# A Mamba scan on one Trainium2 core: decays double-buffered in SBUF, the product with B single-buffered in PSUM

## The chip, the cores and the metric

The kernel runs on 1 core of one Trainium2 chip. The metric is the device time of one execution in microseconds (us). Durations in the text come from one profiled execution; the time is given as the median of three runs.

## The reference, cut to what matters

The network has four parts. The change lies in the third, a selective scan over 4 batches of length 1024 with 512 channels (4 blocks of 128) and 16 states:

```python
dt = softplus(dbl[..., :16] @ W_dt.T + b_dt)
A = -exp(A_log)
def step(h, inp):                       # one position
    dA = exp(dt_t[:, :, None] * A)      # the decay
    h = h * dA + (dt_t * u_t)[:, :, None] * B_t[:, None, :]
    y = einsum('bcs,bs->bc', h, C_t)
ys = scan(step, h0, ...)
y = (ys + u * D_skip) * silu(z)
out = y @ W_out.T
```

`x` here has batch 4, 1024 positions and 256 features. Before the scan come a Fourier-kernel attention block with a gated mix, after it a mixture of 8 experts with layer norm; the change touches neither.

## The kernel before, in words

Two phases follow each other in one program: `phase_a` (attention and mix) and `phase_me` (scan, then experts). In `phase_me` channels lie on the 128 partitions and the 1024 positions along the free axis. One **step** is one state of one block of 128 channels of one batch, so there are 4 batches x 4 blocks x 16 states = 256 steps, numbered n. All engines run their own queues in order and meet at semaphores. A step is:

- **ScalarE, `decay` (L1318 to L1324)**: dA = exp(dt x A) for the 128x1024 tile, into one PSUM buffer `dA`. It waits for `h_ok >= n`, that is, for the scan of step n-1, because that scan reads the one buffer.
- **VectorE, `times_b` (L1610 to L1616)**: dB = du x (row of B, broadcast over the partitions), du read from PSUM, dB written to one of two buffers in SBUF (`late`). It waits for the B row's load, for `du_ok`, and for `h_ok >= n-1`, the scan two steps back.
- **VectorE, `scan` (L1618 to L1623)**: h = scan(dA, dB), into one of three buffers in SBUF. It waits for dA, dB and (from the fourth step) for the product that last read its output buffer.
- **GpSimd, `times_c` (L1144 to L1150)**: pr = h x (row of C).
- **TensorE, `add_state` (L1755 to L1762)**: adds pr onto Y in PSUM by an identity matmul; between these it does `half_job`s, the projections of the same and the next batch (table `FILL`).
- **SyncE, `rows_in` (L1059 to L1067)**: two DMAs a step that broadcast a row of B and a row of C over the partitions; the B row's buffer is freed by `dB_ok`.

The order on VectorE is written out: scan(n), times_b(n+1), scan(n+1), with one `gate` (L1625 to L1630, Y x silu(z)) per block of channels after times_b of the block's third step.

Once per block of 16 steps (t counts the 16 blocks; m is the block within a batch, s the step within the block):

- **GpSimd, `drive` (L1136 to L1142)** makes dt x u for the next block in SBUF (`dus`), at s = 10, 13, 13 and 14 for m = 0 to 3 (table `DRIVE`), behind `times_c` and the work in `besides` (`rate` L1134, `silu` L1130 and, in batches 1 and 2, an indirect DMA at every odd step, L1197).
- **ScalarE, `drive_out` (L1326 to L1330)** copies it to PSUM as `du`, where `times_b` reads it. It waits for `dus_ok`, and for `dB_ok >= 16 t`, the last `times_b` of the block before. It stands at s = 15, after that step's decay and before that step's other jobs.
- **ScalarE, `skip_term` (L1332 to L1338)** writes D x u into Y, at s = `SKIP` = 2, after the decay and after the gate of the block before.
- `block0` to `block3` (L1340 to L1452) are ScalarE's other jobs by step: evacuations of TensorE's half jobs (L1266 to L1292) and the parts of silu and softplus (L1302 to L1316). They stand behind that step's decay.

PSUM holds four tensors of 128x1024 float32: Q0 (dA), Q1 (du), Q2 (the half jobs' two halves), Q3 (Y).

Of the kernel before, what the change touches and what calls it, by code (L numbers as in the profile page):

```python
# [9 lines left out]
ALU = mybir.AluOpType  # L10
ACT = mybir.ActivationFunctionType
AX = mybir.AxisListType

B, L, D = 4, 1024, 256
# [810 lines left out]
DI, NS, DC, DR = 512, 16, 4, 16  # L825
KI = DI // P
STEPS = KI * NS
NBB, NCB, NH, NU = 3, 4, 3, KI + 1
# [65 lines left out]


DRIVE = (10, 13, 13, 14)
SKIP = 2

NTILE = 39
GROUP = 3  # L900
# [4 lines left out]
def phase_me(nc, g):  # L905

    AT = half_jobs()
    with ExitStack() as ctx:
        def sb(name, shape, dt=F32):
            return ctx.enter_context(nc.sbuf_tensor(name, shape, dt))  # L910

        def sem(name):
            return ctx.enter_context(nc.semaphore(name))
# [3 lines left out]
        late = sb("late", [P, 10 * L])  # L917

        def part(of, at, shape, dt=F32):

            n = int(np.prod(shape))
            v = of[:, at:at + n]
            v = v if dt is F32 else v.bitcast(dt)
            if len(shape) == 2:
                return v.rearrange("p (a b) -> p a b", b=shape[1])
            if len(shape) == 3:
                return v.rearrange("p (a b c) -> p a b c", b=shape[1], c=shape[2])
            return v
# [6 lines left out]
        bb = part(rows, NCB * L, [NBB, L])  # L935
        soft = part(rows, 7 * L, [L])
        h = part(late, 0, [NH, L])
        pr = part(late, 3 * L, [NH, L])
        dB = part(late, 6 * L, [2, L])
        dt = part(late, 8 * L, [2, L])  # L940

        w_bc, w_dt, acol, taps, vecs, one, ident = (g[n] for n in ("w_bc", "w_dt", "acol", "taps", "vecs", "one", "ident_m"))
# [54 lines left out]

        Q = [ctx.enter_context(nc.psum_tensor(f"m_Q{i}", [P, 2, CH], F32)) for i in range(4)]
        pT1, pM1, pM2, pT2 = Q
        dA, du, _, Y = (q[:, :, :].rearrange("p a b -> p (a b)") for q in Q)  # L1000
        X = [Q[2][:, i, :] for i in range(2)]
        R0, R1 = Q[3][:, 0, :], Q[3][:, 1, :]

# [7 lines left out]
        dA_ok = sem("m_dA_ok"); dB_ok = sem("m_dB_ok")  # L1011
        h_ok = sem("m_h_ok"); pr_ok = sem("m_pr_ok"); y_full = sem("m_y_full"); yg_ok = sem("m_yg_ok")
# [16 lines left out]
        with nc.Block() as block:  # L1029
# [220 lines left out]
            def _(ac):  # L1250
                A = nc.scalar.activation
# [66 lines left out]
                def decay(b, i):  # L1318
                    n = b * STEPS + i
                    m = i // NS  # L1320
                    ac.wait_ge(dt_ok, b * KI + m + 1)
                    if n:
                        ac.wait_ge(h_ok, n)
                    A(dA[:, :], dt[:, (b * KI + m) % 2, :], ACT.Exp, scale=acol[:, m, i % NS:i % NS + 1]).then_inc(dA_ok, 1)  # L1324

                def drive_out(t):  # L1326
                    ac.wait_ge(dus_ok, t + 1)
                    if t:
                        ac.wait_ge(dB_ok, t * NS)
                    A(du[:, :], dus[:, :], ACT.Identity).then_inc(du_ok, 1)  # L1330

                def skip_term(t):  # L1332

                    if t:
                        ac.wait_ge(yg_ok, t)
                    else:
                        ac.wait_ge(rt_ok, 1)
                    A(Y[:, :], u[:, t % NU, :], ACT.Identity, scale=vecs[:, 1, t % KI:t % KI + 1]).then_inc(skip_ok, 1)  # L1338

                def block0(b, s):  # L1340
                    t = b * KI
                    if b == 0:
                        if s in (1, 2):
                            evacuate(0, "z", 0, s - 1)
                        elif s in (6, 7, 8, 9, 10, 11):
                            evacuate(0, "z", (s - 4) // 2, s % 2)
                        for first, z in ((2, 0), (8, 1), (11, 2), (14, 3)):
                            if 0 <= s - first < 3:
                                sigmoid(0, "z", z, s - first)
                    if s == 0 and b:  # L1350
                        sigmoid(b, "z", 3, 2)
                    elif s in (4, 5):
                        evacuate(b, "dt", 1, s - 4)
                    elif s == 6:
                        softplus(t + 1, 0)
                    if s in (7, 9, 11, 13) and b:
                        evacuate(b - 1, "out", 0, (s - 7) // 2)
                    if s == 7:
                        softplus(t + 1, 1)
                    if s in (14, 15) and b + 1 < B:  # L1360
                        evacuate(b + 1, "x", 0, s - 14)

                def block1(b, s):
                    t = b * KI + 1
                    more = b + 1 < B
                    if s == 0 and b == 0:
                        sigmoid(0, "z", 3, 2)
                    if s in (5, 6):
                        evacuate(b, "dt", 2, s - 5)
                    if more:  # L1370
                        if s == 1:
                            evacuate(b + 1, "conv", 0, 0)
                        elif s == 4:
                            evacuate(b + 1, "conv", 0, 1)
                            sigmoid(b + 1, "conv", 0, 0)
                        elif s in (7, 8):
                            evacuate(b + 1, "z", 0, s - 7)
                        elif s == 9:
                            evacuate(b + 1, "x", 1, 0)
                            sigmoid(b + 1, "conv", 0, 1)  # L1380
                        elif s == 10:
                            evacuate(b + 1, "x", 1, 1)
                            sigmoid(b + 1, "conv", 0, 2)
                        elif s == 11:
                            sigmoid(b + 1, "z", 0, 0)
                        elif s == 12:
                            evacuate(b + 1, "conv", 1, 0)
                            sigmoid(b + 1, "z", 0, 1)
                        elif s == 13:
                            sigmoid(b + 1, "z", 0, 2)  # L1390
                        elif s == 14:
                            evacuate(b + 1, "conv", 1, 1)
                            sigmoid(b + 1, "conv", 1, 0)
                        elif s == 15:
                            evacuate(b + 1, "z", 1, 0)
                            sigmoid(b + 1, "conv", 1, 1)
                    if s == 7:
                        softplus(t + 1, 0)
                    elif s == 8:
                        softplus(t + 1, 1)  # L1400
# [63 lines left out]
                for b in range(B):  # L1464
                    for i in range(STEPS):
                        decay(b, i)
                        m, s = divmod(i, NS)
                        if s == NS - 1 and b * KI + m + 1 < B * KI:
                            drive_out(b * KI + m + 1)
                        if s == SKIP:  # L1470
                            skip_term(b * KI + m)
                        if m == 0:
                            block0(b, s)
                        elif m == 1:
                            block1(b, s)
                        elif m == 2:
                            block2(b, s)
                        elif b + 1 < B:
                            block3(b, s)
# [51 lines left out]
            def _(dv):  # L1531
                v_ = nc.vector
# [77 lines left out]
                def times_b(n):  # L1610
                    t = n // NS
                    dv.wait_ge(b_in[n % NBB], 16 * (n // NBB) + 16)
                    dv.wait_ge(du_ok, t + 1)
                    if n >= 2:
                        dv.wait_ge(h_ok, n - 1)
                    v_.tensor_tensor(dB[:, n % 2, :], du[:, :], bb[:, n % NBB, :], ALU.mult).then_inc(dB_ok, 1)  # L1616

                def scan(n):  # L1618
                    dv.wait_ge(dA_ok, n + 1)
                    dv.wait_ge(dB_ok, n + 1)  # L1620
                    if n >= NH:
                        dv.wait_ge(pr_ok, n - NH + 1)
                    v_.tensor_tensor_scan(h[:, n % NH, :], dA[:, :], dB[:, n % 2, :], 0.0, ALU.mult, ALU.add).then_inc(h_ok, 1)  # L1623

                def gate(t):  # L1625
                    dv.wait_ge(y_full, (t + 1) * NS)
# [4 lines left out]

                route()
                times_b(0)
                for n in range(B * STEPS):
                    scan(n)
# [284 lines left out]
```

## Time and profile before

| | |
|---|---|
| median of 3 runs | 2482.49 us (2481.26 to 2482.85) |
| the profiled execution's own time | 2483.26 us |
| its span, first to last instruction | 2481.1 us |
| scan stage, first to last scan's start | 1063.8 to 2020.4 us |
| busy in the span | PE 1995.6, DVE 1646.6, ACT 1264.7, POOL 1082.0 us |

DVE is VectorE, ACT ScalarE, POOL GpSimd, PE TensorE, SP SyncE; L1623 is line 1623 of the kernel. A row of the timeline gives start, duration, engine, line, operation and tiles (`out<-in`); brackets give the idle time before it and who ended it. A wait is put down to the one that came last, and only idle time over a small threshold is named. Tiles are named by their memory: `late` and `rows` are SBUF tensors that are shared by many buffers, `m_Q` is any of the four PSUM tensors.

### The profile page before, as it was taken

The page shows a single profiled execution, that of the slowest core. Times are in us where ns is not written, and L with a number is a line of the kernel's source. Part 1 is how long each engine was busy: PE and PEld are TensorE (multiplying, and loading weights), DVE is VectorE, ACT ScalarE, POOL GpSimd, SP SyncE. Part 2 cuts the span into 40 slices and gives each one's busy share as a digit, 9 for nine tenths or more (in the row PEclk, how much of TensorE's full clock was granted, in tenths as well). Part 3 has the DMA queues.
Part 4 walks back from the last instruction along what each step waited for, and adds up shares of the span by engine and source line. Part 5 has one row for each costly group of instructions (what it writes and reads, how often), then busy time and mean ns, then how long its engine had stood idle before and what let it go on. Part 6 is the DMA issues. An engine that isn't in the chain of part 4 may idle for free. (4 is left out here: it accounts for less than half of the span.)

```text
span 2481.1 us, 24432 instructions
## 1 busy us (share of the span) xinstructions
PE 1995.6 (80%) x7355; PEld 1006.8 (41%) x7371; DVE 1646.6 (66%) x2303; ACT 1264.7 (51%) x1703; POOL 1082.0 (44%) x605
## 2 busy tenths in 40 slices
PE   4789778967886796879978988998776669989883
PEld 3326433633463253323324332433232236655552
DVE  4754576366726533379989998999899962225663
ACT  3962586268527731466654665466544424434441
POOL 3001201020111010178888898989877751213553
PEclk9899899989999998989998998999999999999996
DMA  7410730073016202488888888988889972223444
GB/s 173 108 34 0 184 72 18 13 189 70 0 38 164 53 34 62 7 286 287 291 288 284 300 275 279 298 289 276 273 274 345 328 255 79 90 89 90 122 122 131
DMA packets 183457, 407.69 MB, mean 164 GB/s; under 512 B 49937, under 2 KB 78865, under 8 KB 182114
## 3 DMA queue, kind: packets, MB, share of 16 engines
q1 hardware_dynamic: 171298, 375.31, 50.3%
q0 software_dynamic: 12032, 30.82, 4.3%
q8 instruction: 63, 1.03, 0.2%
q14 instruction: 64, 0.52, 0.1%
HBM read 360.50 MB, written 49.70 MB: 165 GB/s over the span
## 5 line engine op out<-in xcount | busy, mean ns | idle before, releaser
L1150 POOL TENSOR_TENSOR late<-late,rows 128x1024 f32<-128x1024 f32 x256 | 603.2, 2361 | 153.6 <-DVE late L1623 148.4
L1760 PE MATMUL m_Q<-late,ident_m 128*128 128x512 f32 x1024 | 527.7, 646 | 170.7 <-POOL late L1150 118.2
L1623 DVE TENSOR_TENSOR_SCAN late<-m_Q,late 128x1024 f32<-128x1024 f32 x256 | 586.3, 2290 | 47.5 <-ACT m_Q L1324 19.5
L1324 ACT ACTIVATE m_Q<-late,acol 128x1024 f32<-128x1024 f32 x256 | 286.0, 1117 | 373.9 <-DVE late L1623 373.7
L1760 PEld LDWEIGHTS m_Q<-late,ident_m 128*128 128x128 f32 x1024 | 193.1, 201 | 478.2 <-POOL late L1150 281.7
L1616 DVE TENSOR_TENSOR late<-m_Q,rows 128x1024 f32<-128x1024 f32 x256 | 307.3, 1200 | 40.5 <-ACT m_Q L1330 34.5
L424 DVE SCALAR_TENSOR_TENSOR early<-early,work 128x1024 f32<-128x1024 f32 x128 | 156.0, 1219 | 123.1 <-ACT early L570 122.3
L1507 ACT ACTIVATE late<-m_Q,e_b1c 128x128 f32<-128x128 f32 x312 | 89.2, 369 | 202.4 <-PE m_Q L1825 173.2
L302 POOL TENSOR_TENSOR xk<-kr 128x1024 f32<-128x1024 f32 x8 | 15.0, 1894 | 397.3 <-DVE kr L438 397.3
L570 ACT ACTIVATE early<-work,rnd 128x1024 f32<-128x1024 f32 x128 | 141.7, 1110 | 63.2 <-PE work L722 60.0
L1837 PE MATMUL m_Q<-rows,late 128*128 x624 | 155.8, 393 | 21.3 <-ACT late L1507 12.5
L277 POOL TENSOR_TENSOR qkh<-early,qkh 128x1024 bf16<-128x1024 f32 x16 | 33.9, 2129 | 284.4 <-ACT qkh L533 284.4
L1816 PE MATMUL m_Q<-early,late 128*128 x312 | 151.8, 610 | 2.6 <-ACT late L1491 2.0
L578 ACT ACTIVATE early<-early,halfpi 128x1024 f32<-128x1024 f32 x128 | 146.0, 1141 | 0.0
L577 ACT ACTIVATE early<-early 128x1024 f32<-128x1024 f32 x128 | 134.8, 1053 | 21.1 <-DVE early L427 21.0
L1837 PEld LDWEIGHTS m_Q<-rows,late 128*128 128x128 f32 x624 | 112.7, 190 | 52.2 <-issue 39.9
L1728 PE MATMUL m_Q<-early 128*128 128x512 f32 x256 | 122.5, 605 | 4.8 <-ACT m_xi L1266 4.0
L465 DVE TENSOR_TENSOR s<-work,s 128x1024 f32<-128x1024 f32 x8 | 9.8, 1225 | 172.9 <-PE work L646 172.9
L646 PE MATMUL work<-w,qkh 128*128 128x256 f32 x512 | 112.6, 381 | 10.9 <-ACT qkh L594 10.9
L1733 PE MATMUL m_Q<-m_xi,early 128*128 128x512 f32 x256 | 119.7, 601 | 0.0
L1651 DVE TENSOR_TENSOR late<-m_Q,m_u 128x256 f32<-128x256 f32 x39 | 16.6, 425 | 144.4 <-PE m_Q L1837 105.2
L808 PE MATMUL work<-x2T,w 128*128 128x512 f32 x256 | 111.6, 594 | 1.0 <-ACT x2T L510 1.0
(226 smaller groups left out, 3086.5 us busy)
## 6 DMA issues: line engine op xcount, KB each, us to landing
rows<-bc_s SPq DMA_DIRECT2D x512, 512.0 KB, 5.5
stack<-st_s SPq DMA_DIRECT2D x64, 384.0 KB, 5.8
st_s<-qkh SPq DMA_DIRECT2D x128, 96.0 KB, 2.4
r_s<-late SPq DMA_DIRECT2D x39, 256.0 KB
stack<-st_s SPq DMA_DIRECT2D x32, 256.0 KB, 6.7
xin<-in_x SPq DMA_DIRECT2D x4, 1024.0 KB, 9.9
xres<-in_x SPq DMA_DIRECT2D x4, 1024.0 KB, 7.5
mx_s<-s SPq DMA_DIRECT2D x4, 1024.0 KB, 4.5
```

The costliest lines, as they stand in the source:

```text
L424: v_.scalar_tensor_tensor(fs[:, s % 3, :], fs[:, s % 3, :], ROUND, slot(b, *job)[:, :], ALU.subtract, ALU.subtract).then_inc(rr_ok, 1)
L570: A(fs[:, s % 3, :], slot(b, *job)[:, :], ACT.Identity, bias=rnd[:, :]).then_inc(turns_ok, 1)
L577: A(fs[:, s % 3, :], fs[:, s % 3, :], ACT.Sin, scale=-TURN).then_inc(feat_ok, 1)
L578: A(fc[:, s % 3, :], fc[:, s % 3, :], ACT.Sin, scale=-TURN, bias=halfpi[:, :]).then_inc(feat_ok, 1)
L1150: nc.gpsimd.tensor_tensor(pr[:, n % NH, :], h[:, n % NH, :], cb[:, n % NCB, :], ALU.mult).then_inc(pr_ok, 1)
L1324: A(dA[:, :], dt[:, (b * KI + m) % 2, :], ACT.Exp, scale=acol[:, m, i % NS:i % NS + 1]).then_inc(dA_ok, 1)
L1616: v_.tensor_tensor(dB[:, n % 2, :], du[:, :], bb[:, n % NBB, :], ALU.mult).then_inc(dB_ok, 1)
L1623: v_.tensor_tensor_scan(h[:, n % NH, :], dA[:, :], dB[:, n % 2, :], 0.0, ALU.mult, ALU.add).then_inc(h_ok, 1)
L1728: ins = mm(dst[:, :], w_in[:, k, (m + KI * (kind == "z")) * P:(m + KI * (kind == "z") + 1) * P], half(xT[:, k, :], c), start=(k == 0), sto ...
L1760: ins = mm(half(Y, c), ident[:, :], half(pr[:, n % NH, :], c), start=False, stop=(n % NS == NS - 1), skip_group_check=True)
L1816: ins = mm(pM1[:, q % 2, :], xsT[:, q % 2, k * P:(k + 1) * P], e_w1[:, k, bass.ds(e * HE, HE)], start=(k == 0), stop=(k == KD - 1))
L1837: ins = mm(pM2[:, q % 2, 0:D], hT[:, q % 2, k * P:(k + 1) * P], e_w2[:, k, bass.ds(e * D, D)], start=(k == 0), stop=(k == HE // P - 1 and ...
```

## The change

The decays get two buffers in SBUF, the place where dB had its two; dB gets the one PSUM buffer where the decays were. The waits follow the buffers. `skip_term` moves from s = 2 to s = 3, and `drive_out` from s = 15 (after the block's last decay) to s = 0 of the next block (after that block's first decay).

```diff
-SKIP = 2
+SKIP = 3
...
-        dB = part(late, 6 * L, [2, L])
+        dA = part(late, 6 * L, [2, L])
...
-        dA, du, _, Y = (q[:, :, :].rearrange("p a b -> p (a b)") for q in Q)
+        dB, du, _, Y = (q[:, :, :].rearrange("p a b -> p (a b)") for q in Q)
...
                     ac.wait_ge(dt_ok, b * KI + m + 1)
-                    if n:
-                        ac.wait_ge(h_ok, n)
-                    A(dA[:, :], dt[:, (b * KI + m) % 2, :], ACT.Exp, scale=acol[:, m, i % NS:i % NS + 1]).then_inc(dA_ok, 1)
+                    if n >= 2:
+                        ac.wait_ge(h_ok, n - 1)
+                    A(dA[:, n % 2, :], dt[:, (b * KI + m) % 2, :], ACT.Exp, scale=acol[:, m, i % NS:i % NS + 1]).then_inc(dA_ok, 1)
...
                         m, s = divmod(i, NS)
-                        if s == NS - 1 and b * KI + m + 1 < B * KI:
-                            drive_out(b * KI + m + 1)
+                        if s == 0 and b * KI + m:
+                            drive_out(b * KI + m)
                         if s == SKIP:
                             skip_term(b * KI + m)
...
                     dv.wait_ge(du_ok, t + 1)
-                    if n >= 2:
-                        dv.wait_ge(h_ok, n - 1)
-                    v_.tensor_tensor(dB[:, n % 2, :], du[:, :], bb[:, n % NBB, :], ALU.mult).then_inc(dB_ok, 1)
+                    if n:
+                        dv.wait_ge(h_ok, n)
+                    v_.tensor_tensor(dB[:, :], du[:, :], bb[:, n % NBB, :], ALU.mult).then_inc(dB_ok, 1)
...
-                    v_.tensor_tensor_scan(h[:, n % NH, :], dA[:, :], dB[:, n % 2, :], 0.0, ALU.mult, ALU.add).then_inc(h_ok, 1)
+                    v_.tensor_tensor_scan(h[:, n % NH, :], dA[:, n % 2, :], dB[:, :], 0.0, ALU.mult, ALU.add).then_inc(h_ok, 1)
```

## Rows read from the trace of the kernel before

**Rows 1.** Groups by line, whole span: count, busy us, mean ns, idle before, releaser
```profile
L1623 DVE TENSOR_TENSOR_SCAN late<-m_Q,late 128x1024 f32<-128x1024 f32 x256 | 586.3, 2290 | 47.5 <-ACT m_Q L1324 19.5
L1616 DVE TENSOR_TENSOR late<-m_Q,rows 128x1024 f32<-128x1024 f32 x256 | 307.3, 1200 | 40.5 <-ACT m_Q L1330 34.5 <-DMA rows<-bc_s 6.0
L1324 ACT ACTIVATE m_Q<-late,acol 128x1024 f32<-128x1024 f32 x256 | 286.0, 1117 | 373.9 <-DVE late L1623 373.7
```

**Rows 2.** The line of the scan: shortest, median, longest; first and last start
```profile
L1623 DVE TENSOR_TENSOR_SCAN late<-m_Q,late x256: 2283/2291/2293, 1063.8 to 2020.4; 128x1024 f32<-128x1024 f32 x128
```

**Rows 3.** Timeline of an ordinary step: start us, duration us
```profile
1408.52 1.20 DVE L1616 TENSOR_TENSOR late<-m_Q,rows 128x1024 f32<-128x1024 f32 x1
1408.70 1.12 ACT L1324 ACTIVATE m_Q<-late,acol 128x1024 f32<-128x1024 f32 x1 [0.77 <-DVE late L1623]
1409.85 2.29 DVE L1623 TENSOR_TENSOR_SCAN late<-m_Q,late 128x1024 f32<-128x1024 f32 x1
1412.06 1.20 DVE L1616 TENSOR_TENSOR late<-m_Q,rows 128x1024 f32<-128x1024 f32 x1
1413.39 2.29 DVE L1623 TENSOR_TENSOR_SCAN late<-m_Q,late 128x1024 f32<-128x1024 f32 x1
```

**Rows 4.** Timeline of a step whose B row came late
```profile
1105.21 1.12 ACT L1324 ACTIVATE m_Q<-late,acol 128x1024 f32<-128x1024 f32 x1 [0.96 <-DVE late L1623]
1107.81 1.23 DVE L1616 TENSOR_TENSOR late<-m_Q,rows 128x1024 f32<-128x1024 f32 x1 [2.70 <-DMA rows<-bc_s]
1109.13 2.29 DVE L1623 TENSOR_TENSOR_SCAN late<-m_Q,late 128x1024 f32<-128x1024 f32 x1
```

**Rows 5.** Timeline in the first phase: the second waits for the first
```profile
300.71 1.22 DVE L424 SCALAR_TENSOR_TENSOR early<-early,work 128x1024 f32<-128x1024 f32 x1 [1.30 <-ACT early L570]
301.96 0.69 DVE L427 TENSOR_SCALAR early<-early 128x1024 int32<-128x1024 int32 x1
```

**Rows 6.** Groups by line and form, ScalarE and VectorE
```profile
L1330 ACT ACTIVATE m_Q<-dus 128x1024 f32<-128x1024 f32 x16 | 16.4, 1028 | 33.9 <-POOL dus L1142 33.6
L1308 ACT ACTIVATE early<-early 128x1024 f32<-128x1024 f32 x32 | 33.5, 1046 | 0.1
L396 DVE SCALAR_TENSOR_TENSOR early<-work,cols,qkh 128x1024 f32<-128x1024 f32 x16 | 20.5, 1283 | 54.0 <-ACT qkh L529 36.2 <-issue 17.8
```

**Rows 7.** Timeline before block 7 (steps 107 to 112), GpSimd, ScalarE, VectorE
```profile
1466.66 2.39 POOL L1150 TENSOR_TENSOR late<-late,rows 128x1024 f32<-128x1024 f32 x1 [1.14 <-DVE late L1623]
...
1478.40 2.37 POOL L1142 TENSOR_TENSOR dus<-late,m_u 128x1024 f32<-128x1024 f32 x1
1480.80 1.03 ACT L1330 ACTIVATE m_Q<-dus 128x1024 f32<-128x1024 f32 x1 [2.49 <-POOL dus L1142]
1481.91 1.23 DVE L1616 TENSOR_TENSOR late<-m_Q,rows 128x1024 f32<-128x1024 f32 x1 [1.28 <-ACT m_Q L1330]
1484.56 2.29 DVE L1623 TENSOR_TENSOR_SCAN late<-m_Q,late 128x1024 f32<-128x1024 f32 x1 [1.42 <-ACT m_Q L1324]
```

**Rows 8.** Timeline before block 8 (steps 125 to 128)
```profile
1534.32 2.36 POOL L1150 TENSOR_TENSOR late<-late,rows 128x1024 f32<-128x1024 f32 x1 [1.15 <-DVE late L1623]
...
1542.46 2.34 POOL L1142 TENSOR_TENSOR dus<-late,m_u 128x1024 f32<-128x1024 f32 x1
1545.95 1.23 DVE L1616 TENSOR_TENSOR late<-m_Q,rows 128x1024 f32<-128x1024 f32 x1 [4.73 <-ACT m_Q L1330]
1547.97 2.29 DVE L1623 TENSOR_TENSOR_SCAN late<-m_Q,late 128x1024 f32<-128x1024 f32 x1 [0.79 <-ACT m_Q L1324]
```

**Rows 9.** Timeline before block 6 (steps 94 to 96)
```profile
1415.30 0.69 ACT L1271 ACTIVATE m_u<-m_Q,vecs 128x512 f32<-128x512 f32 x1 [1.95 <-PE m_Q L1733]
1424.09 2.29 DVE L1623 TENSOR_TENSOR_SCAN late<-m_Q,late 128x1024 f32<-128x1024 f32 x1 [1.28 <-ACT m_Q L1324]
```

**Rows 10.** Timeline, steps 79 and 80: the half job that a copy at s = 15 waits for
```profile
1357.44 1.88 PE L1728 MATMUL m_Q<-early 128*128 128x512 f32 x4
```

**Rows 11.** Waits of VectorE from 1060 to 2030 us: total, times, longest
```profile
DVE late L1623 <- ACT m_Q L1324: 19.5, 25, 2.4
```

## The prediction

> **What bounds the kernel now.** I read three views: the groups by line, the timeline of VectorE beside its suppliers, and the waits. The groups first [rows 1]: the 256 scans of 2290 ns and the 256 `times_b` of 1200 ns are 893.6 us of VectorE work, in a stage of 2020.4 - 1063.8 = 956.6 us from the first to the last scan's start [rows 2]. VectorE is the engine of this stage. The difference is what a change of waits can touch: 16 gates of about 0.92 us each in the chain, and small gaps and stalls.
>
> The timeline of an ordinary step shows more than the groups' idle column [rows 3]. A scan starts at 1409.85 and lasts 2.29 us, but the next `times_b` starts 2.21 us after it: it waits for nothing that is recent, and starts 0.08 us before the scan's end. The next scan starts 1.33 us after the `times_b` start, though that lasted 1.20. So a step takes 3.54 us (3.535 over several), and 211 of the 255 intervals between scans show this to 0.02 us. Two waits end nearly together ahead of the scan: the decay's end (1408.70 + 1.12 = 1409.82, and the scan starts 0.03 later), and `times_b`'s own completion. ScalarE cannot start the decay before the last scan ended, which is why it waits 373.7 us [rows 1].
>
> Which of the two holds the scan is told by the one step whose B row was late [rows 4]. There the decay had ended at 1106.33, far ahead, and the scan still started 1109.13 - 1107.81 = 1.32 us after `times_b`, that is 0.09 us after the end of that 1.23 us instruction. VectorE waiting for its own last result costs 0.09 us here. With the decay out of the way the leg from `times_b` to scan therefore stays at 1.32 us. It gives back 0.01 us a step, not 0.13.
>
> **The change part by part.**
>
> *Decays in two buffers.* The decay of step n may now start after scan n-2. ScalarE comes off the ordinary step; it gives 0.01 us there, by the paragraph above. Its own length is hidden either way (writing SBUF instead of PSUM costs it about 0.02: 1046 ns SBUF to SBUF against 1028 ns into PSUM [rows 6]). Where a decay was late because of ScalarE's other jobs, the lead of a whole step covers it. The waits give 19.5 us in 25 cases [rows 11]. Ten of them stand at the turn of a block and are priced below: three like the 0.79 of rows 8, three like the 1.42 of rows 7, and two each like the 1.28 of rows 9 and the 1.3 of the step before it, together 11.8. One more, 2.2, is a decay behind a copy that itself waits for TensorE; it keeps its place behind that copy and stays. About 5.5 us in 14 cases are left, of which 0.13 each is the gap that is there anyway. Gain: 3.7 us.
>
> *The product in one buffer.* `times_b` of step n+1 must not overwrite dB before scan n has read it, so its wait becomes `h_ok >= n+1` in effect: VectorE waits for the scan that it has just issued. The 0.08 us overlap is lost and a wait for its own result is added. No row shows this pair. Nearest is rows 4, the same two lines in the other order, with other waits beside the own one on both instructions: 0.09. The other end is the link in the first phase, where the second waits for the first and starts 301.96 - 300.71 - 1.22 = 0.03 us after its end [rows 5]. I take 0.09: scan start to `times_b` start becomes 2.29 + 0.09 = 2.38, from 2.21.
>
> *`times_b` writes PSUM.* No VectorE instruction of the trace writes PSUM. ScalarE's nearest pair is 0.02 us cheaper into PSUM [rows 6]. VectorE's two-input instructions of 1024 columns lie between 1.20 and 1.28 us [rows 1, 6], so I bound it by 0.06 either way and take -0.02. The scan reads one operand from PSUM and one from SBUF before and after: nothing.
>
> *The ordinary step* is then 2.38 + 1.32 - 0.02 = 3.68 us against 3.535: +0.145. Queued behind the waiting `times_b` is only VectorE's own scan; behind that are GpSimd and TensorE, which follow at the same distance. The DMAs of the B rows are released by `dB_ok` as before and get more time. A step with a gate loses the same overlap once.
>
> *Where GpSimd sets the time.* Ahead of eight blocks `drive` on GpSimd is late; beside the first block's fill these are most of the waits for L1330 in rows 1. The longer step hides behind them. Before block 8 [rows 8] GpSimd works without a pause from 1534.32 to 1544.80, then comes `drive_out`, and `times_b` starts at 1545.95. Before the change ScalarE then still had a silu part and the decay to do, and the scan started at 1547.97. With `drive_out` moved behind the decay of the new block, that decay is done meanwhile, while VectorE waits its 4.73 us: scan at 1545.95 + 1.30 = 1547.25, 0.72 earlier. Three such places: -2.2. Before block 7 [rows 7] GpSimd is busy from 1466.66 to 1480.77; the scan would start at 1481.91 + 1.30 = 1483.21 instead of 1484.56: -1.35, and before block 11, the same place in the next batch, as much: -2.7; in the first batch, where the indirect DMAs are missing, some -0.8. Before block 6 (twice) a copy at s = 14 waits 1.95 us for TensorE [rows 9], and after it the order is copy, silu part, decay, `drive_out`, so du gets later while the decay gets earlier; between -0.2 and -1.2 each, I take -0.7: -1.4. Sum -7.1 us, and about 35 of the 255 intervals lie in these stretches and don't pay the 0.145.
>
> *`drive_out` one step later.* Where GpSimd is in time (blocks 1, 5, 9), du now stands behind a copy of x that needs TensorE's half job of step 78, 1357.44 + 1.88 = 1359.32 [rows 10], then 0.6 for the copy, 1.12 for the decay and 1.03 for itself: about 1362.1, and `times_b` could have started at about 1361.5. The slower steps give GpSimd and TensorE 0.145 a step to catch up. I take 0; bound 0.6 each.
>
> *`skip_term` one step later.* It stood behind the decay that starts after scan 16t+1, and still does, since that is now the decay of s = 3. It waits for the gate as before. Nothing.
>
> *Sum:* 220 x 0.145 = 31.9, less 7.1, less 3.7: +21.1 us. Against the profiled execution's 2483.26 (span 2481.1 and 2.2 around it) this is 2504.4; the median of the runs lies 0.8 below, so 2503.6, rounded to 2504.
>
> **The rivals.** A change of 0.2% (5 us) is about what a measurement of this kernel can tell from none.
>
> *The own wait is cheap behind a scan*, 0.03 as in rows 5. The step is 3.62, +0.085: 18.7 - 10.8 = +8, so 2490. For it speaks that rows 5 is also a wait for its own last result; against it that the waits in this loop come in threes, as at rows 4, where it cost 0.09. Chance 0.12.
>
> *Faster:* if the overlap is no real gain, and the scan's end would have held `times_b` anyway, the new wait is free. The step is 2.21 + 1.30 = 3.51, 220 x -0.025 - 10.8 = -16, so 2466. It decides if scan to `times_b` stays under about 2.27 us: there 220 x 0.05 is eaten by the 10.8 of gains. Against it stands the 2.21 of rows 3, shorter than the scan itself, which an instruction that waits for the scan's completion can't have. Chance 0.10. The Trainium skill has this as a rule, in "VectorE: DVE Perf Modes", section "The DRAIN you can't avoid": the next VectorE instruction does not start until the pipe is empty, and a semaphore after each "costs nothing extra". By that rule this change would be free on VectorE and faster; the trace's overlap of 0.08 us without a wait and gap of 0.09 with one disagree.
>
> *No change:* the cheap wait (0.03) together with a PSUM write 0.06 shorter: 3.58 a step, 220 x 0.045 - 10.8 = -1, about 2482. Chance 0.08.
>
> *The new order on ScalarE hurts:* du is late ahead of blocks 1, 5 and 9 by the full 0.6 and the gains before blocks 6 and 10 fail (1.4) with a further 1 us each: +5 on the forecast, 2509. Chance 0.06.
>
> *The PSUM write is dearer* by 0.06 instead of cheaper by 0.02: 220 x 0.08 = +18, so 2521. Chance 0.04.
>
> **How the numbers follow.** The forecast, both own waits at 0.09, has 0.60. The range 2486 to 2520 takes in the forecast, the cheap wait, ScalarE's order and part of the no-change case; outside are the faster case, the dear write and the rest, under 0.2. Slower by over 0.2%: 0.60 + 0.12 + 0.06 + 0.04 = 0.82. Same 0.08, faster 0.10.
>
> **What the profile would show.** Right: scan to `times_b` 2.38 (from 2.21), `times_b` to scan 1.30 to 1.32 (from 1.33), an ordinary step of 3.68 and VectorE's waits for L1324 near zero; ScalarE's decays start over 2 us ahead of their scan; the stretch from first to last scan about 978 us. The wait for L1330 stays at some 30 us in the blocks named. Wrong: a scan to `times_b` time under 2.3, a mean of L1616 away from 1.20 to 1.23 us, or new waits of VectorE for L1330 ahead of blocks 1, 5 and 9.

## The result, and the profile after

The changed kernel takes 2519.86 us in the median (2518.88 to 2521.87, 4 runs) against 2482.67 us before (2481.26 to 2493.47, 4 runs): a ratio of 1.0141, 95% interval 1.0112 to 1.017, 37 us slower. The forecast was 2504, with a range from 2486 to 2520.

The groups by line, from the page of the changed kernel (busy us, mean ns, idle before, releaser), answer to [rows 1]:

```profile
L1623 DVE TENSOR_TENSOR_SCAN late<-late,m_Q 128x1024 f32<-128x1024 f32 x256 | 585.3, 2286 | 23.4 <-DVE m_Q L1616 2.2
L1324 ACT ACTIVATE late<-late,acol 128x1024 f32<-128x1024 f32 x256 | 292.3, 1144 | 236.5 <-DVE late L1623 225.9
L1616 DVE TENSOR_TENSOR m_Q<-m_Q,rows 128x1024 f32<-128x1024 f32 x256 | 315.6, 1233 | 69.9 <-ACT m_Q L1330 32.8
```

VectorE no longer waits for the decay at all: the 19.5 us of [rows 11] are gone (the 2.2 us in the scan's line are put down to `times_b`), and ScalarE waits 225.9 instead of 373.7 us for the scan. That part of the change did what it says. But the idle time ahead of `times_b` has grown from 40.5 to 69.9 us, of which the waits with a name explain no more than before. The line of the scan shows the stage, which answers to [rows 2]:

```profile
L1623 DVE TENSOR_TENSOR_SCAN late<-late,m_Q x256: 2278/2287/2290, 1065.1 to 2054.7; 128x1024 f32<-128x1024 f32 x128
```

From the first to the last scan's start it is 989.6 us, 33.0 more than before. Where they are is plain in an ordinary step of the timeline (start us, duration us), which answers to [rows 3]:

```profile
1200.45 2.29 DVE L1623 TENSOR_TENSOR_SCAN late<-late,m_Q 128x1024 f32<-128x1024 f32 x1
1202.83 1.15 ACT L1324 ACTIVATE late<-late,acol 128x1024 f32<-128x1024 f32 x1 [2.20 <-DVE late L1623]
1202.87 1.23 DVE L1616 TENSOR_TENSOR m_Q<-m_Q,rows 128x1024 f32<-128x1024 f32 x1
1204.19 2.29 DVE L1623 TENSOR_TENSOR_SCAN late<-late,m_Q 128x1024 f32<-128x1024 f32 x1
```

`times_b` starts 2.42 us after the scan (2.21 before), 0.13 us behind its end, and the next scan 1.32 us after `times_b` (1.33 before). The step is 3.74 us instead of 3.54. The decay at 1202.83 belongs to the scan after the one of 1204.19: it is a whole step early.

Ahead of block 8 the gain that the forecast named is there, against [rows 8]; this is the changed kernel's timeline at that place:

```profile
1562.07 1.23 DVE L1616 TENSOR_TENSOR m_Q<-m_Q,rows 128x1024 f32<-128x1024 f32 x1 [4.33 <-ACT m_Q L1330]
1563.40 2.29 DVE L1623 TENSOR_TENSOR_SCAN late<-late,m_Q 128x1024 f32<-128x1024 f32 x1
```

The scan follows `times_b` after 1.33 us, where it took 1547.97 - 1545.95 = 2.02. The three intervals between scans up to it take 15.43 us against 16.11.

The two profiled spans differ by 39.0 us: 33.0 in the stage, 1.3 ahead of it, 4.7 behind the last scan's start. The last two are not the change's: behind the last scan's start the span has 460.7 us before and 465.4 after, but 452.6 in a run below that has the same instructions there (old_order, 2516.2 - 2063.6).

The 33.0 us understate the change a little. The profiled execution of the kernel before has one stall that the runs below don't show, at step 24 (ScalarE's copy, the decay behind it, the scan):

```profile
1152.55 0.60 ACT L1275 ACTIVATE m_zs<-m_Q 128x512 f32<-128x512 f32 x1 [3.55 <-PE m_Q L1728]
1153.99 1.11 ACT L1324 ACTIVATE m_Q<-late,acol 128x1024 f32<-128x1024 f32 x1
1155.13 2.29 DVE L1623 TENSOR_TENSOR_SCAN late<-m_Q,late 128x1024 f32<-128x1024 f32 x1 [2.38 <-ACT m_Q L1324]
```

That interval takes 5.79 us, 2.25 over an ordinary one. TensorE's granted clock was 0.51 there, from 1146 to 1152 us, the 1.2 GHz level, and ScalarE's copy waited for its half job. The kernel own_first_b below has the same buffers and the same ScalarE order, had a clock of 1.00 in that stretch and loses nothing at step 24. Without this stall the stage before would be some 954.4 us (an estimate, 956.6 - 2.25) and the change's loss in it 35.2.

### The profile page after: what moved, and what is told of

Its sections match the earlier page's. It is cut to its first block, busy times and chain, and to the rows that moved or that the text cites. A ratio compares the mean times of both kernels' runs of the same rounds, so it can differ in the third digit from the quotient of the medians.

```text
span 2520.1 us, 24431 instructions
## 1 busy us (share of the span) xinstructions
PE 2013.7 (80%) x7355; PEld 1011.4 (40%) x7371; DVE 1675.2 (66%) x2303; ACT 1266.4 (50%) x1703; POOL 1081.2 (43%) x605
## 4 chain that ended last, share of the span: by engine, by line
DVE 29%; PE 17%; POOL 4%; issue 4%; ACT 2%; DMA 1%; another core or an unknown queue 1%; DVEq 1%; ACTq 0%; POOLq 0%; SPq 0%
DVE late L1623 18%; DVE m_Q L1616 10%; PE m_Q L1837 6%; PE m_Q L1816 4%; POOL late L1150 3%; PE m_Q L1760 2%; PE m_Q L1825 2%; PE m_Q L1728 1%; PE m_Q L1733 1%; DVE m_yT L1630 1%; ACT late L1507 1%; POOL dus L1142 1%; PE m_Q L1748 1%; DMA rows<-bc_s 1%
## 5 line engine op out<-in xcount | busy, mean ns | idle before, releaser
L1760 PE MATMUL m_Q<-late,ident_m 128*128 128x512 f32 x1024 | 540.0, 660 | 194.2 <-POOL late L1150 124.8
L1623 DVE TENSOR_TENSOR_SCAN late<-late,m_Q 128x1024 f32<-128x1024 f32 x256 | 585.3, 2286 | 23.4 <-DVE m_Q L1616 2.2
L1324 ACT ACTIVATE late<-late,acol 128x1024 f32<-128x1024 f32 x256 | 292.3, 1144 | 236.5 <-DVE late L1623 225.9
L1616 DVE TENSOR_TENSOR m_Q<-m_Q,rows 128x1024 f32<-128x1024 f32 x256 | 315.6, 1233 | 69.9 <-ACT m_Q L1330 32.8
L1837 PE MATMUL m_Q<-rows,late 128*128 x624 | 162.8, 406 | 24.1 <-ACT late L1507 12.3
L465 DVE TENSOR_TENSOR s<-work,s 128x1024 f32<-128x1024 f32 x8 | 9.8, 1225 | 172.9 <-PE work L646 172.9
```

Of the source, the lines that this page charges most:

```text
L1324: A(dA[:, n % 2, :], dt[:, (b * KI + m) % 2, :], ACT.Exp, scale=acol[:, m, i % NS:i % NS + 1]).then_inc(dA_ok, 1)
L1616: v_.tensor_tensor(dB[:, :], du[:, :], bb[:, n % NBB, :], ALU.mult).then_inc(dB_ok, 1)
L1623: v_.tensor_tensor_scan(h[:, n % NH, :], dA[:, n % 2, :], dB[:, :], 0.0, ALU.mult, ALU.add).then_inc(h_ok, 1)
L1760: ins = mm(half(Y, c), ident[:, :], half(pr[:, n % NH, :], c), start=False, stop=(n % NS == NS - 1), skip_group_check=True)
L1837: ins = mm(pM2[:, q % 2, 0:D], hT[:, q % 2, k * P:(k + 1) * P], e_w2[:, k, bass.ds(e * D, D)], start=(k == 0), stop=(k == HE // P - 1 and ...
```

## The experiments

Times are medians. The first four ran on one chip (before: 2480.31 us), the second four on one (before: 2483.86 us), the last two on another (before: 2462.19 us). Their traces are shorter behind the last scan, 441.4 and 439.1 us against 452.6 to 466.2 elsewhere, so that of these only the ratio and the stage are compared. The stage is that of one profiled execution.

| kernel | us | ratio to before, 95% interval | scan to `times_b` | `times_b` to scan | step | stage us |
|---|---|---|---|---|---|---|
| before | | 1 | 2.21 | 1.33 | 3.54 | 956.6 |
| the change | 2519.86 | 1.0141 (1.0112 to 1.017) | 2.42 | 1.32 | 3.74 | 989.6 |
| wait_only | 2522.91 | 1.0168 (1.0134 to 1.0201) | 2.42 | 1.31 | 3.74 | 996.2 |
| own_first | 2488.36 | 1.0027 (1.0012 to 1.0042) | 2.32 | 1.27 | 3.59 | 957.5 |
| old_order | 2522.91 | 1.0168 (1.0137 to 1.0199) | 2.42 | 1.32 | 3.74 | 997.6 |
| both_two | 2656.83 | 1.0698 (1.066 to 1.0735) | 2.20 and 3.43 by turns | 1.29 | 3.49 and 4.7 by turns | 1122.3 |
| own_first_b | 2494.7 | 1.0045 (1.0028 to 1.0062) | 2.21 | 1.38 | 3.59 | 965.5 |
| du_sbuf | 2673.83 | 1.0768 (1.0744 to 1.0792) | 2.20 | 1.30 and more | from 3.50 | 1147.2 |
| late_drive | 2479.89 | 0.9982 (0.9965 to 0.9999) | 2.21 | 1.33 | 3.54 | 949.7 |
| late_drive_early | 2476.95 | 0.9973 (0.9961 to 0.9986) | 2.21 | 1.33 | 3.54 | 944.0 |
| own_middle | 2488.18 | 1.0106 (1.0088 to 1.0124) | 2.38 | 1.32 | 3.70 | 981.5 |
| own_first_early | 2462.93 | 1.0005 (0.9996 to 1.0014) | 2.32 | 1.27 | 3.59 | 955.5 |

### wait_only: the wait without the placing

The kernel before, with the stricter wait alone.

```diff
-                    if n >= 2:
-                        dv.wait_ge(h_ok, n - 1)
+                    if n:
+                        dv.wait_ge(h_ok, n)
```

> The kernel before with one wait made stricter: times_b of step n waits for scan n-1 instead of n-2; all buffers stay where they were. Theory (VectorE's wait for the scan that it has just issued costs the time): the scan's start to the next times_b's start goes from 2.21 to 2.42 us, as in the changed kernel, and the leg from there to the scan gets longer than 1.32 only if something else holds it. A step of 3.73 us; 220 x 0.195 = +43 us, some 2525 us. Rival (the placing of dB in PSUM costs it): 2.21 and 3.54 us stay, 2482 us.

2522.91 us, 1.0168. An ordinary step of its timeline:

```profile
1241.74 2.29 DVE L1623 TENSOR_TENSOR_SCAN late<-m_Q,late 128x1024 f32<-128x1024 f32 x1
1244.13 1.12 ACT L1324 ACTIVATE m_Q<-late,acol 128x1024 f32<-128x1024 f32 x1 [2.62 <-DVE late L1623]
1244.17 1.23 DVE L1616 TENSOR_TENSOR late<-m_Q,rows 128x1024 f32<-128x1024 f32 x1
1245.48 2.29 DVE L1623 TENSOR_TENSOR_SCAN late<-m_Q,late 128x1024 f32<-128x1024 f32 x1
```

The same 2.42 us to a hundredth, with every buffer where it was: the wait is the whole loss of the ordinary step. The decay is late again (1244.13, after the scan) and still ready in time, since `times_b` now ends later too. The placing shows only in `times_b`'s length: 1233 ns into PSUM, 1225 ns here into SBUF. The 1200 ns of [rows 1] and this 1225 are the same instruction, without and with a wait that ends just ahead of it, as in the 1.23 of [rows 4].

### own_first: the order of the wait statements

```diff
 def times_b(n):
     t = n // NS
+    if n:
+        dv.wait_ge(h_ok, n)
     dv.wait_ge(b_in[n % NBB], 16 * (n // NBB) + 16)
     dv.wait_ge(du_ok, t + 1)
-    if n:
-        dv.wait_ge(h_ok, n)
...
 def scan(n):
-    dv.wait_ge(dA_ok, n + 1)
     dv.wait_ge(dB_ok, n + 1)
+    dv.wait_ge(dA_ok, n + 1)
```

> The changed kernel with the order of VectorE's wait statements turned round: the wait for its own last result stands first on times_b and on the scan, those for the loads, du, the decay and the product behind it. Theory A (the 0.09 and 0.13 us after an own result are the way over a separate wait instruction, which carries the own wait when it isn't the first): both gaps fall towards the 0.03 us of the first phase's links, a step of 3.58 to 3.62 instead of 3.74 us, 2485 to 2495 us. Rival B (the gap is the engine's own, whatever the order): step 3.74 us, 2520 us.

2488.36 us, 1.0027. Its timeline:

```profile
1241.78 2.29 DVE L1623 TENSOR_TENSOR_SCAN late<-late,m_Q 128x1024 f32<-128x1024 f32 x1
1244.10 1.23 DVE L1616 TENSOR_TENSOR m_Q<-m_Q,rows 128x1024 f32<-128x1024 f32 x1
1245.37 2.29 DVE L1623 TENSOR_TENSOR_SCAN late<-late,m_Q 128x1024 f32<-128x1024 f32 x1
```

Both gaps are 0.03 to 0.04 us now: 2.32 and 1.27 us from start to start. Theory A held, and three quarters of what the ordinary step had lost (0.15 of 0.20 us) was in the order of statements. In the recorded trace (the views above leave such instructions out) the semaphore of an instruction's first wait stands on the instruction itself, and the other two stand on one instruction of the sequencer ahead of it; a wait that ends last is cheapest on the instruction. The rest stays: a wait that the kernel before doesn't have costs 0.03 us plus the lost overlap of 0.08.

The quicker step also shows a price of the new place of `drive_out` that the slow step had hidden: `times_b` now waits 0.34, 0.26 and 0.28 us for it ahead of blocks 1, 5 and 9.

### own_middle: the forecast's missing 0.04 us

```diff
     dv.wait_ge(b_in[n % NBB], 16 * (n // NBB) + 16)
-    dv.wait_ge(du_ok, t + 1)
     if n:
         dv.wait_ge(h_ok, n)
+    dv.wait_ge(du_ok, t + 1)
```

> The changed kernel with times_b's three waits in the order B row, scan, du instead of B row, du, scan. Theory (the gap after an own result depends on the wait's place in the list: 0.03 us where it is the first, 0.13 where it is the last of three as on times_b, 0.09 where it is the middle one as on the scan; the forecast's missing 0.04 us is this): scan to times_b 2.38 instead of 2.42, a step of 3.70, 220 x 0.04 = 9 us less, 2511 us. Rival (0.13 belongs to the pair scan then times_b, whose longer instruction or PSUM input costs more): 2.42 and 3.74 us stay, 2520 us.

Ratio 1.0106 (1.0088 to 1.0124), with a step of 3.70; this is its timeline:

```profile
1241.06 2.29 DVE L1623 TENSOR_TENSOR_SCAN late<-late,m_Q 128x1024 f32<-128x1024 f32 x1
1243.44 1.23 DVE L1616 TENSOR_TENSOR m_Q<-m_Q,rows 128x1024 f32<-128x1024 f32 x1
1244.76 2.29 DVE L1623 TENSOR_TENSOR_SCAN late<-late,m_Q 128x1024 f32<-128x1024 f32 x1
```

2.38 us, as expected to the hundredth. So the place in the list of three costs 0.03 (first), 0.09 (middle) or 0.13 us (last) behind the release.

### own_first_b: the turn of the scan's list in the kernel before

```diff
 def scan(n):
-    dv.wait_ge(dA_ok, n + 1)
     dv.wait_ge(dB_ok, n + 1)
+    dv.wait_ge(dA_ok, n + 1)
```

> The kernel before, with the scan's wait for its own engine's product placed ahead of its wait for the decay, nothing else. In the changed kernel the same turn took the leg from times_b to scan from 1.32 to 1.27 us. Theory (before the change ScalarE's decay, which ends 0.03 us ahead of the scan, would hold the scan anyway, so the decay's lead is needed to profit): 1.33 and 3.54 us stay, 2480 us, no difference. Rival (only the own wait held it): 1.27 us, a step of 3.48, 12 us faster.

2494.7 us, 1.0045: neither. `times_b` to scan went from 1.33 up to 1.38, the step to 3.59:

```profile
1239.03 1.20 DVE L1616 TENSOR_TENSOR late<-m_Q,rows 128x1024 f32<-128x1024 f32 x1
1239.20 1.12 ACT L1324 ACTIVATE m_Q<-late,acol 128x1024 f32<-128x1024 f32 x1 [2.47 <-DVE late L1623]
1240.41 2.29 DVE L1623 TENSOR_TENSOR_SCAN late<-m_Q,late 128x1024 f32<-128x1024 f32 x1 [0.18 <-DVE late L1616]
```

The decay ends at 1240.32 and the scan starts 0.09 us later, where it was 0.03 in [rows 3]. The decay is what held the scan before, and its wait has now lost the place on the instruction: it costs 0.06 us more. (The bracket names `times_b`, which had ended 0.18 before.) That confirms the reading of [rows 3], and shows that the place matters for the wait that ends last, an engine's own or not.

### old_order: ScalarE's order undone

```diff
-SKIP = 3
+SKIP = 2
...
-                        if s == 0 and b * KI + m:
-                            drive_out(b * KI + m)
+                        if s == NS - 1 and b * KI + m + 1 < B * KI:
+                            drive_out(b * KI + m + 1)
```

> The changed kernel with ScalarE's drive_out and skip_term back at their old steps (15 and 2). Theory (moving drive_out behind the new block's first decay gave back about 0.7 us ahead of blocks 4, 8 and 12 and 1.3 ahead of 7 and 11): those intervals get longer by 0.7 to 1.3 us each, 3 to 7 us in all, 2523 to 2527 us, the ordinary step stays 3.74. Rival (a decay that leads by a step makes the order meaningless): 2520 us.

2522.91 us; its interval overlaps the change's, so the times alone don't tell them apart. The intervals between scans do: up to the first scan of blocks 3, 4, 6, 7, 8, 10, 11 and 12 they are 4.34, 7.44, 5.96, 5.57, 8.66, 5.95, 5.57 and 8.66 us, against 3.74, 6.71, 5.19, 4.23, 7.94, 5.17, 4.23 and 7.94 in the changed kernel, 7.0 us in all. The stage is 997.6 against 989.6 us. Without the order, the lead of the decays and dB's place in PSUM are together worth nothing over wait_only (996.2).

### late_drive, late_drive_early: the order alone, on the kernel before

```diff
                         m, s = divmod(i, NS)
-                        if s == NS - 1 and b * KI + m + 1 < B * KI:
-                            drive_out(b * KI + m + 1)
                         ...
                         elif b + 1 < B:
                             block3(b, s)
+                        if s == NS - 1 and b * KI + m + 1 < B * KI:
+                            drive_out(b * KI + m + 1)
```

> The kernel before with one move on ScalarE: drive_out stands behind the other jobs of the block's last step instead of ahead of them. Theory (what the change gained at the blocks' turns came from ScalarE's order alone, since it leaves nothing but the decay between du and the next scan): ahead of blocks 3, 4, 7, 8, 11, 12 the interval shrinks by 0.7 to 1.4 us, ahead of 6 and 10 by about 1, 6 to 9 us in all, ordinary step 3.54: 2473 us. Rival (the gain needs the decays' lead): 2480 us.

2479.89 us against 2483.86, 0.9982 (0.9965 to 0.9999), the stage 949.7 us, of whose 6.9 us less 2.25 are the stall of step 24. The place of [rows 7] in this kernel:

```profile
1477.52 1.03 ACT L1330 ACTIVATE m_Q<-dus 128x1024 f32<-128x1024 f32 x1 [0.76 <-POOL dus L1142]
1478.49 1.10 ACT L1324 ACTIVATE m_Q<-late,acol 128x1024 f32<-128x1024 f32 x1
1478.64 1.22 DVE L1616 TENSOR_TENSOR late<-m_Q,rows 128x1024 f32<-128x1024 f32 x1 [1.25 <-ACT m_Q L1330]
1479.95 2.29 DVE L1623 TENSOR_TENSOR_SCAN late<-m_Q,late 128x1024 f32<-128x1024 f32 x1
```

The copy and the silu part now lie in ScalarE's wait for GpSimd; only the decay is left behind du, beside `times_b`. The scan comes 1.31 us after `times_b`, where it was 2.65. Over the eight turns, each from the scan that GpSimd last waited for to the first scan of the block, the intervals take 8.2 us less than before, in the changed kernel 6.5. So what the change won at the turns needs no second decay buffer. The time is nevertheless the one that the rival named, because four steps (102, 104, 166 and 168) got 3.5 us longer in all: their decay stands behind a copy that waits for TensorE. The second run also moves GpSimd's work:

```diff
-DRIVE = (10, 13, 13, 14)
+DRIVE = (10, 12, 12, 13)
```

> The run before this with GpSimd's drive one step earlier for m = 1, 2 and 3 (steps 12, 12, 13 instead of 13, 13, 14), as early as rate allows. du is ready one times_c (2.36 us) earlier ahead of blocks 4, 8 and 12, and earlier by that and an indirect DMA elsewhere. If GpSimd's lateness is all that is left there, 3 x 2.3 us and some 3 x 0.7 us go: 2464 us. Rival (GpSimd's later products then hold the scan through h's three buffers): 2473 us.

2476.95 us, 0.9973 (0.9961 to 0.9986): faster than both kernels, by less than expected. The waits of VectorE for du fell, those for the decay rose (late_drive first, then this run; total us, times, longest):

```profile
DVE late L1616 <- ACT m_Q L1330: 36.9, 11, 16.6
DVE late L1623 <- ACT m_Q L1324: 8.2, 14, 1.1
```

```profile
DVE late L1616 <- ACT m_Q L1330: 27.4, 11, 16.6
DVE late L1623 <- ACT m_Q L1324: 12.6, 17, 1.9
```

Of 9.5 us, 4.4 came back as waits for the decay. Its trace says what holds ScalarE there, here at step 49:

```profile
1245.16 0.60 ACT L1275 ACTIVATE m_zs<-m_Q 128x512 f32<-128x512 f32 x1 [3.01 <-PE m_Q L1728]
1245.65 1.14 ACT L1305 ACTIVATE early<-early,one 128x1024 f32<-128x1024 f32 x1
1246.69 1.11 ACT L1324 ACTIVATE m_Q<-late,acol 128x1024 f32<-128x1024 f32 x1
1247.83 2.29 DVE L1623 TENSOR_TENSOR_SCAN late<-m_Q,late 128x1024 f32<-128x1024 f32 x1 [1.92 <-ACT m_Q L1324]
```

With du earlier, the next step's copy waits for TensorE's half job instead, and the decay waits behind the copy. ScalarE's waits at that copy, late_drive first, then this run:

```profile
ACT m_zs L1275 <- PE m_Q L1728: 5.0, 4, 1.8
ACT m_zs L1275 <- PE m_Q L1728: 14.2, 12, 3.0
```

The next limit at these places is TensorE; no run moves its half jobs.

### own_first_early: the best of the change

The changed kernel with both turned lists of own_first and the DRIVE of the run above.

> The changed kernel with the own waits first (3.59 us a step, 2488 us in its run) and GpSimd's drive one step earlier for m = 1 to 3. Theory (what is left at the blocks' turns is du's lateness): ahead of blocks 4, 8 and 12 2.3 us less each, ahead of 6, 7, 10, 11 about 1 less, 8 to 11 us in all, 2479 us, level with the kernel before. Rival (as in the kernel before with the same step, where part came back as new stalls): 2485 us.

Ratio 1.0005 (0.9996 to 1.0014): level with the kernel before. Its stage is 955.5 us against 956.6, or against some 954.4 without the stall of step 24: the turns give back all but about 1 us of what the 0.05 us of each step cost. It stays behind late_drive_early (0.9973, stage 944.0); the two ran on different chips.

### both_two, du_sbuf: why the change pays with a wait at all

both_two gives dB its second buffer back, in SBUF (the edits that make room for it are left out here):

```diff
...
-                    if n:
-                        dv.wait_ge(h_ok, n)
-                    v_.tensor_tensor(dB[:, :], du[:, :], bb[:, n % NBB, :], ALU.mult).then_inc(dB_ok, 1)
+                    if n >= 2:
+                        dv.wait_ge(h_ok, n - 1)
+                    v_.tensor_tensor(dBs[n % 2][:, :], du[:, :], bb[:, n % NBB, :], ALU.mult).then_inc(dB_ok, 1)
...
```

> The changed kernel with two buffers for dB as well (one in PSUM, one in SBUF) and times_b waiting for the scan two steps back, as before the change; the B and C rows' staging tile shares memory with the output tile to make room. Theory: the leg from scan to times_b is 2.21 us again and that from times_b to scan 1.32, a step of 3.53, and the gains at the blocks' turns stay: 15 us below the kernel before, some 2467 us. Rival (the decay's lead and the new order are worth nothing): 2482 us.

2656.83 us, 1.0698. This was 190 us off. The groups of its VectorE in the scan stage, kept apart by form, name the reason:

```profile
L1628 DVE TENSOR_TENSOR_SCAN late<-late 128x1024 f32<-128x1024 f32 x128 | 464.1, 3626 | 15.7 <-ACT late L1329 2.5 <-POOL late L1152 2.0 <-issue 0.4
L1628 DVE TENSOR_TENSOR_SCAN late<-late,m_Q 128x1024 f32<-128x1024 f32 x128 | 292.4, 2284 | 14.0 <-ACT late L1329 3.9 <-issue 0.4
```

A scan with one operand in PSUM takes 2284 ns; with both in SBUF, 3626 ns in the mean. Its timeline shows what they wait for, VectorE first, then GpSimd:

```profile
1483.39 8.11 DVE L1628 TENSOR_TENSOR_SCAN late<-late 128x1024 f32<-128x1024 f32 x1
...
1624.52 2.29 DVE L1628 TENSOR_TENSOR_SCAN late<-late 128x1024 f32<-128x1024 f32 x1
```

```profile
1482.39 2.38 POOL L1144 TENSOR_TENSOR dus<-late,m_u 128x1024 f32<-128x1024 f32 x1
1484.70 2.35 POOL L1152 TENSOR_TENSOR late<-late,rows 128x1024 f32<-128x1024 f32 x1
1487.00 2.35 POOL L1132 TENSOR_TENSOR m_zs<-m_zs,early 128x1024 f32<-128x1024 f32 x1
...
1624.69 2.92 POOL L1199 DMA_INDIRECT ext_s<-ent,pos  x1 [0.17 <-issue]
```

The scan of 1483.39 lasts 8.11 us: GpSimd is at work without a pause until 1489.35, and the scan ends 2.15 us later, one scan's length. The scan of 1624.52 found GpSimd idle and took its 2.29; there GpSimd's indirect DMA took 2.92 instead of the 1.0 of the kernel before. The Trainium skill has the rule in "SBUF — State Buffer", section "SBUF: two separate sides": a VectorE instruction with two SBUF inputs and a GpSimd instruction that reads SBUF ask for the same port pair, and the one that comes second "fully blocks". The trace agrees in both directions, with one difference: the section gives the pair to whichever starts first, but the GpSimd instructions of 1484.70 and 1487.00 started after the scan of 1483.39 and still went ahead of it.

du_sbuf tests the same on `times_b`: du is read where GpSimd wrote it, `drive_out` is gone, dB has two PSUM buffers.

```diff
...
-                    v_.tensor_tensor(dB[:, :], du[:, :], bb[:, n % NBB, :], ALU.mult).then_inc(dB_ok, 1)
+                    v_.tensor_tensor(dBs[n % 2][:, :], dus[:, t % 2, :], bb[:, n % NBB, :], ALU.mult).then_inc(dB_ok, 1)
...
```

> The changed kernel with du read from SBUF where GpSimd wrote it (two buffers) and drive_out left out, which frees two PSUM banks: dB gets two buffers, both in PSUM, and times_b waits for the scan two steps back. Every scan reads one operand from PSUM, but times_b reads both from SBUF. Theory (a VectorE instruction with both inputs in SBUF is held up by GpSimd's work, as the 3.6 us scans of the run with dB in both places suggest): scans stay at 2.29 us, times_b grows by 0.5 us or more in the mean, a step over 3.9 us, 2560 us or more. Rival (those long scans came of something that is only in a scan, or of ScalarE's writes): times_b 1.22 us, a step of 3.53, about 2465 us.

2673.83 us, 1.0768, as the theory said; the groups in its scan stage:

```profile
L1618 DVE TENSOR_TENSOR_SCAN late<-late,m_Q 128x1024 f32<-128x1024 f32 x256 | 585.3, 2286 | 23.4 <-issue 1.8 <-ACT late L1328 0.4
L1611 DVE TENSOR_TENSOR m_Q<-dus,rows 128x1024 f32<-128x1024 f32 x256 | 534.9, 2089 | 27.7 <-POOL dus L1143 23.3 <-DMA rows<-bc_s 4.4
```

The scans are back at 2286 ns, and `times_b` has grown from 1233 to 2089 in the mean; the rival, that only a scan or ScalarE's writes were the matter, is out. So each scan and each `times_b` of this kernel needs one operand in PSUM while GpSimd works, and three of the four PSUM tensors are taken by du, Y and the half jobs. If the fourth is dA, ScalarE has no lead; if it is dB, VectorE waits for itself. The change swapped one for the other, and both kernels that avoid it were slower for the port.

## Why the prediction was right in direction, and what it missed

- **The own wait costs more than the decays' lead gives.** Right, and shown by wait_only and own_first. The forecast step of 3.68 was 3.74: scan to `times_b` 2.42 for 2.38, since the gap of 0.09 was taken over from the scan's list, where the own wait stands in the middle, to `times_b`'s, where it stands last (own_middle shows the 0.04); and `times_b` to scan 1.32 for 1.30.
- **The PSUM write at -0.02 us** is the term of the sum with the wrong sign: +0.01 (1233 against 1225 ns). ScalarE's pair was no guide for VectorE. The two together are 0.06 a step, 220 x 0.06 = 13 us, against the 11.9 by which the stage's 33.0 exceed the forecast's 21.1. That these two figures are so close is luck: other terms were off too and cancel. The turns gave 0.6 and the late decays 1.8 us less than forecast, and the pauses named below cost 0.9; against that stand the 2.2 of step 24 and 2.4 us less of waits for B rows, which the forecast said would get more time and did not price.
- **The decay holds the ordinary step by 0.01 us only.** The number came out, 1.32 with a decay a step early, but the reading of [rows 4] mixed two things. In both_two, where the decay is early and `times_b` takes its 1.20 us, the scan follows `times_b` after 1.29: the decay held the kernel before by 0.04 us. In the change `times_b` itself takes 1.23, as it did in [rows 4], since a wait now ends just ahead of it, and that takes 0.03 back.
- **The turns of blocks.** Each is measured from the scan that GpSimd last waited for. Ahead of block 8, three intervals, -0.68 for -0.72; ahead of block 7, five intervals of 20.37 became 19.20, -1.16 for -1.35; ahead of block 6, seven intervals, -0.8 for -0.7; ahead of block 3, four intervals, -0.6 for -0.8. In all -6.5 for -7.1. No new wait ahead of blocks 1, 5 and 9.
- **3.7 us from decays that were late.** Half wrong: 1.9. Five of these places (the intervals of 3.85 before at steps 23, 54, 85, 116 and 147) are not ScalarE's: they stand at the same steps in the changed kernel, as 4.10, where no decay is late. At step 23 of the kernel before the decay had ended at 1149.00, 0.34 us ahead of the scan that is said to wait for it:

```profile
1147.88 1.12 ACT L1324 ACTIVATE m_Q<-late,acol 128x1024 f32<-128x1024 f32 x1 [0.84 <-DVE late L1623]
1149.34 2.29 DVE L1623 TENSOR_TENSOR_SCAN late<-m_Q,late 128x1024 f32<-128x1024 f32 x1 [0.44 <-ACT m_Q L1324]
```

  They come 31 steps apart, which is 128 instructions of VectorE's queue each time, its sequencer's included. In own_first and own_first_early no interval at these steps is longer than its neighbours. What the pauses are was not tested.
- **A decay behind TensorE's half job "stays" (2.2 us).** It didn't: this is the stall of step 24. In the changed kernel the copy still waits 1.51 us there and the decay's lead covers it; but own_first_b, without a lead, has no such wait, so the 2.2 belong to that one execution and are not shown to be a gain of the change.
- **The rivals.** The cheap wait, 0.03, is what the first place in the list gives (own_first, a step of 3.59 and 2488 us for the 3.62 and 2490 that the rival priced, though by an order that the change doesn't have). The faster rival, that the wait costs VectorE nothing, is refuted by wait_only: some 40 us for one stricter wait. The section of the Trainium skill that the prediction names for it ("VectorE: DVE Perf Modes", "The DRAIN you can't avoid") also says that a next instruction "that is not held starts earlier", which the prediction left out; the overlap of 0.08 us agrees with that half of it, and only "costs nothing extra" disagrees with the runs.
- **The range** held the time by 0.1 us, which is luck: two of the four runs lie outside it, at 2520.34 and 2521.87. Its upper end should have carried both unknown terms at their ends.

## What to carry to other kernels

On an engine that bounds a stage, look at the distance from start to start: an instruction that doesn't wait for the one just issued started 0.08 us before its end here, and a wait for it costs 0.11 to 0.21 us by its place, in a column that shows no idle time with a name. Where such a wait can't be avoided, put the wait that ends last first in the list. Before a tile moves out of PSUM, see whether the VectorE instructions that read it keep an operand there while GpSimd works; and where an engine waits for a late input, put its other jobs ahead of the copy, not behind.

## What the runs showed of the hardware that was not expected

- The place of a wait in the list of an instruction's three: 0.03, 0.09 or 0.13 us from the end of the instruction waited for to the start, for the same pair of instructions (own_first, own_middle, the change).
- A scan with both inputs in SBUF beside GpSimd takes 3626 ns in the mean and up to 8.12 us, alone 2.29 (both_two); a two-input multiply 2089 ns in the mean for 1233 (du_sbuf). A scan that GpSimd holds up is not let in between GpSimd instructions that follow without a pause.
- VectorE's write to PSUM instead of SBUF costs 8 ns on 128x1024 (1233 against 1225 ns, the change and wait_only); ScalarE's exponential with a scale per partition took 1117 ns into PSUM and 1144 into SBUF.
- A pause of 0.31 to 0.36 us in VectorE's queue every 31 steps, which is every 128 of its instructions; not seen where its own waits stand first in both lists (own_first, own_first_early). Its cause is open.
